# Feed-forward in front of an attention block: where eight 768 KB copies of constant rows are issued

## The chip, the cores and the metric

The kernel runs on one core of one Trainium2 chip. The metric is device time in microseconds (us), taken per execution. The time of before is the median of three runs. A profile comes from one further execution; its span leaves out a little of what the device time holds.

## What is computed

The input x is four sequences of 512 tokens of 128 numbers. The reference runs two layers of the form feed-forward, attention, feed-forward. The change lies in the first block of the first layer:

```
x = x + 0.5 * L0_ffn(layernorm(x))
x = x + L0_attn(layernorm(x))
...
```

`L0_ffn` sends each token to one of eight experts. The router takes a softmax over eight logits and the largest one wins. The chosen expert computes `gelu(t @ w1[e] + b1[e]) @ w2[e] + b2[e]`, which is multiplied by the winner's probability. `L0_attn` has 16 heads of 8 numbers with relative positions: besides q·k the scores get terms that depend on the distance of query and key in blocks of 64. The far part of these terms is put into the matmul: each head's q and k get 24 further rows. Some of them are the same for every input, zeros and ones that mark blocks of positions ("constant rows").

## The kernel before, in words

`network` (L2442) runs the phases in order. `constants_phase` starts the loads of x. `ffn_phase` (L306, its tiles are named l0f) is the first feed-forward. `relative_attend` (l0am) is the attention. Then come the second feed-forward, and the spline and causal phases of layer 1.

`ffn_phase` has two parts. In the first, the router: VectorE (DVE) normalises and ranks the 2048 tokens, and GpSimd (POOL) writes them sorted by expert to the DRAM tensor `sorted_tokens`, with 16 indirect DMAs (L499), then eight more that blank the rows past each expert's last token (L504). In the second part 23 slots of 128 tokens are worked through. For each slot s:

- SyncE (SP) reads the slot's row from SBUF (`packed_of`, L415), then copies the expert's w1 to `mine` (`load_mine`, L461, 256 KB) and loads the slot's tokens into `xs` (`load_tokens`, L471, 64.5 KB). For the first eight slots `load_tokens` waits for the slot's blanking DMA (`blanked[s]`).
- TensorE (PE) transposes the tokens (L872), does four "up" products (L882) and later four "down" products (L893). ScalarE (ACT) applies gelu (L593). DVE copies (L764) and adds the bias (L774), POOL writes the result to `token_results` (L509).

SP issues `mine` and `xs` four slots ahead (AHEAD = 4). The first four are outside the loop, the loop's body s issues those of slot s + 4.

While this phase runs, the attention's weights are prepared (`AttentionWeights`, the argument `aside`, tiles l0w). SP loads them behind the expert weights (`aside.load`, L953). PE, DVE and ACT form `wext` and `row_bias` between router and slots (`multiply`, L977: L981 to L1000). SP also stores the constant rows: `store_blocks` (L961) is one DMA from DRAM to DRAM of 16 heads x 24 rows x 512 numbers, 768 KB, for one sequence and side (q or k). There are eight, B = 4 sequences x 2 sides. The kernel before issues one at the end of the loop's bodies 0 to 7. `store_edges` (L969) follows behind the loop. The attention waits for all ten at L1237, behind its first row products.

The DMAs that SP issues share one queue (q1), on the same 16 DMA engines as POOL's indirect ones (q0). The order of the work is written out by hand: each engine runs its instructions in the order of the code and waits on semaphores.

Of the kernel before, what the change touches and what calls it, by code (L numbers as in the profile page):

```python
# [15 lines left out]
B, S, D = 4, 512, 128  # L16
# [289 lines left out]
def ffn_phase(nc, kept, name, x, arrivals, consts, w, scratch_dram, aside=None, late=None, closing=None):  # L306
# [4 lines left out]
    with ExitStack() as ctx:  # L311
        own_sems = []

        def sb(n, shape, dt=F32):
            return ctx.enter_context(nc.sbuf_tensor(f"{name}_{n}", shape, dt))
# [13 lines left out]
            return [sem(f"{n}{j}") for j in range(UNROLL)]  # L329

        SETS = TILES // 4
        experts = sb("experts", [P, EXPERTS, SLAB])
        mine = sb("mine", [P, UNROLL, FF])
        b1 = sb("b1", [EXPERTS * FC, P])
# [17 lines left out]
        onehot_b = sb("onehot_b", [P, TILES, EXPERTS], BF16)  # L352
        next_row = sb("next_row", [P, SETS, EXPERTS])
        place = sb("place", [P, TILES, EXPERTS])
# [58 lines left out]
        def packed_of(engine, s):  # L413

            return engine.value_load(packed_i[0:1, s:s + 1], min_val=0, max_val=EXPERTS * (XS_ROWS - P) + EXPERTS - 1)  # L415

        def row_of(packed):
            return (packed >> OWNER_BITS).with_bounds(max_val=XS_ROWS - P)

        def part_of(packed, at, n):  # L420
            expert = (packed & (EXPERTS - 1)).with_bounds(min_val=0, max_val=EXPERTS - 1)
            return experts[:, bass.ds(expert, 1), at:at + n].rearrange("p a k -> p (a k)")

        def load_results(queue, first, end):

            for j in range(UNROLL):
                queue.wait_ge(ys_out[j], 16 * len(range(j, SLOTS, UNROLL)))
            for b in range(first, end):
                queue.dma_start(yg[:, 4 * b:4 * b + 4, :], ys_dram[512 * b:512 * b + 512, :].rearrange("(t p) d -> p t d", p=P))\
                    .then_inc(gathered[b], 16)  # L430

        with nc.Block() as block:

            @block.sync
            def _(sp):
                sp.dma_start(switch_w[:, :], w["switch_w"]).then_inc(switch_in, 16)
                sp.dma_start(switch_b[:, :], w["switch_b"].unsqueeze(0).partition_broadcast(P)).then_inc(switch_in, 16)
                loads = [
                    (b1[:, :], w["b1"].rearrange("e (k p) -> (e k) p", p=P)),
                    (experts[:, :, SLAB_W1:SLAB_W2], w["w1"].rearrange("e d f -> d e f")),  # L440
                    (experts[:, :, SLAB_B2:SLAB_B1], w["b2"].unsqueeze(0).partition_broadcast(P)),
                ]
                for dst, src in loads:
                    sp.dma_start(dst, src).then_inc(weights_in, 16)
                for e in range(EXPERTS):
                    sp.dma_start(experts[:, e, SLAB_W2:SLAB_B2].rearrange("p (k d) -> p k d", k=FC),
                                 w["w2"][e].rearrange("(k p) d -> p k d", p=P)).then_inc(weights_in, 16)
                if aside:
                    aside.load(sp)
                if late:  # L450
                    late.load(sp)
                sp.wait_ge(weights_in, FFN_LOADS * 16)
                sp.wait_ge(b1_ready, 1)
                sp.wait_ge(rows_ready, 1)

                def load_mine(s, row):

                    j = s % UNROLL
                    if s >= UNROLL:
                        sp.wait_ge(up_ready, s - UNROLL + 1)  # L460
                    sp.dma_start(mine[:, j, :], part_of(row, SLAB_W1, FF)).then_inc(mine_in[j], 16)  # L461

                def load_tokens(s, row):

                    j = s % UNROLL
                    if s < EXPERTS:
                        sp.wait_ge(blanked[s], 16)
                    if s >= UNROLL:
                        sp.wait_ge(xsT_psum, s - UNROLL + 1)
                        sp.wait_ge(tokens_ready, s - UNROLL + 1)  # L470
                    sp.dma_start(xs[:, j, 0:XS_COLS], xs_dram[bass.ds(row_of(row), P), :]).then_inc(xs_in[j], 16)  # L471

                rows = [packed_of(sp, s) for s in range(AHEAD)]
                for s in range(AHEAD):
                    load_mine(s, rows[s])
                if arrivals:
                    sp.wait_ge(arrivals[1], 16)
                sp.wait_ge(scattered, 16 * TILES)
                for s in range(AHEAD):
                    load_tokens(s, rows[s])  # L480
                for s in range(SLOTS):
                    if s + AHEAD < SLOTS:
                        row = packed_of(sp, s + AHEAD)
                        load_mine(s + AHEAD, row)
                        load_tokens(s + AHEAD, row)
                    if aside and s < 2 * B:
                        aside.store_blocks(sp, s)
                if aside:
                    aside.store_edges(sp)
                load_results(sp, 0, B // 2)  # L490
# [110 lines left out]
            def _(dve):  # L601
# [126 lines left out]

                last_rows = next_row[:, SETS - 1, :]
                done(dve.tensor_scalar(blank_pos[:, :], last_rows, c["own_row"][:, 0:1], None, ALU.add))  # L730
# [1711 lines left out]
def network(nc, inputs, out, tables):  # L2442

    def weights(prefix, *more):
        names = {n[len(prefix):]: a for n, a in inputs.items() if n.startswith(prefix)}
        return {**names, **{n: tables[n] for n in more}}


    sorted_tokens = nc.dram_tensor("sorted_tokens", (XS_ROWS, XS_COLS), F32).ap()
    token_results = nc.dram_tensor("token_results", (YS_ROWS, D), F32).ap()  # L2450
    with ExitStack() as ctx:
        x = ctx.enter_context(nc.sbuf_tensor("x_tokens", [P, TILES, D], F32))
        c, x_in, empty_out = constants_phase(nc, ctx, x, inputs["L0_attn_hidden_states"], sorted_tokens)
        attention_w, dram = weights("L0_attn_", "own_head", "block_rows"), attention_dram(nc)
        closing = AttentionClosing(nc, ctx, "l0a", x, c, attention_w)
        with ExitStack() as attention_ctx:
            aside = AttentionWeights(nc, attention_ctx, "l0w", c, attention_w, dram)
            with aside.scratch():
                ffn_phase(nc, ctx, "l0f0", x, (x_in, empty_out), c, weights("L0_ffn_"), (sorted_tokens, token_results), aside)
            relative_attend(nc, ctx, "l0am", x, closing.xn, closing.heads, c, aside, closing.weights, dram)  # L2460
        layer1 = LayerOneWeights(nc, ctx, "l1w", c, weights("L1_ffn_"), weights("L1_attn_", "cos_rows", "sin_rows"))
        with layer1.scratch():
            ffn_phase(nc, ctx, "l0f1", x, None, c, weights("L0_ffn_"), (sorted_tokens, token_results), None, layer1, closing)
        spline_phase(nc, "l1f0", x, c, layer1)
        causal_phase(nc, "l1a", x, c, layer1)
        spline_phase(nc, "l1f1", x, c, layer1, out)
# [19 lines left out]
```

## Time and profile before

| what | us |
|---|---|
| median of 3 runs (788.44 to 790.29) | 788.75 |
| the profiled execution's own time | 788.52 |
| its span | 786.8 |
| PE busy over the span | 583.0 |
| DVE busy | 531.2 |
| ACT busy | 437.1 |
| POOL busy | 219.6 |

Times of an instruction or a stretch are us from the span's start. A row of the timeline gives start, duration, engine, line, operation, output and inputs, count, and in brackets the idle time before it with what ended it. SPq stands for the issuing of DMAs by SP: its duration is the issuing, not the transfer. In the rows of stretches a bracket (x4) counts instructions, PEclk is the granted TensorE clock as a share of 2.4 GHz, and the DMA share is the mean busy share of the core's 16 DMA engines (it can pass 1, as packets overlap).

### The profile page before, as it was taken

The numbers are of one execution on the slowest core, as the hardware profiler recorded it, in microseconds if no ns is written. First come the engines' busy times: TensorE is split into PE (matmuls) and PEld (weight loads), VectorE is DVE, ScalarE is ACT, GpSimd is POOL, SyncE is SP. The second block draws the span as 40 slices with busy tenths as digits, with TensorE's granted clock in tenths as the row PEclk, the third lists the DMA queues.
The fourth block names the chain that finished last, engine by engine and source line by source line (L and its number), as shares of the span: only waits on it lengthen the run. The fifth ranks groups of instructions, "written<-read, shape, count | busy, mean of one in ns | idle before, by whom it ended". The sixth has DMA issues, their size and how long they took to land. (4 is left out here: it accounts for less than half of the span.)

```text
span 786.8 us, 16609 instructions
## 1 busy us (share of the span) xinstructions
PE 583.0 (74%) x5220; PEld 417.2 (53%) x5220; DVE 531.2 (68%) x1878; ACT 437.1 (56%) x944; POOL 219.6 (28%) x274
## 2 busy tenths in 40 slices
PE   4499927727999999999999998343993661686660
PEld 3387923324666566667666666233982451364460
DVE  7612235815787678989999995771226888766887
ACT  2034524415888788888888884631551523464522
POOL 1743422000950391095040000056442100212000
PEclk9999977866999999999999998655997655799655
DMA  8669525989989899999954413725552000000001
GB/s 251 179 182 391 185 79 169 289 342 269 283 274 335 220 278 348 324 225 271 338 157 129 124 48 99 165 76 146 180 166 71 0 1 1 0 1 2 0 1 53
DMA packets 133602, 130.79 MB, mean 166 GB/s; under 512 B 29565, under 2 KB 109485, under 8 KB 131853
## 3 DMA queue, kind: packets, MB, share of 16 engines
q1 hardware_dynamic: 126668, 103.61, 46.3%
q0 software_dynamic: 4736, 25.07, 8.7%
q10 hardware_dynamic: 2112, 1.05, 0.5%
q8 instruction: 44, 0.72, 0.4%
q14 instruction: 42, 0.34, 0.1%
HBM read 73.43 MB, written 52.92 MB: 161 GB/s over the span
## 5 line engine op out<-in xcount | busy, mean ns | idle before, releaser
L1442 DVE CUSTOM_DVE_ANT_0 l0am_prob<-l0am_ps_s,l0am_bias 128x512 f32<-128x512 f32 x256 | 161.6, 687 | 56.1 <-PE l0am_ps_s L1519 34.9
L1361 ACT ACTIVATE l0am_prob<-l0am_prob,l0am_neg_top 128x512 f32<-128x512 f32 x256 | 172.1, 730 | 19.1 <-DVE l0am_neg_top L1442 19.0
L1531 PE MATMUL l0am_ps_t<-c_ident,l0am_prob 128*128 128x128 f32 x1024 | 138.2, 279 | 0.0
L1531 PEld LDWEIGHTS l0am_ps_t<-c_ident,l0am_prob 128*128 128x128 f32 x1024 | 113.8, 142 | 16.7 <-issue 16.6
L1355 ACT COPY l0am_probT<-l0am_ps_t 128x512 f32<-128x512 f32 x128 | 69.0, 590 | 45.6 <-PE l0am_ps_t L1531 45.6
L1519 PE MATMUL l0am_ps_s<-l0am_ks,l0am_qs 32*128 32x512 f32 x512 | 74.0, 647 | 21.7 <-DVE l0am_neg_top L1442 19.5
L1429 DVE COPY l0am_probT<-l0am_ps_t 128x512 f32<-128x512 f32 x128 | 82.2, 683 | 2.5 <-PE l0am_ps_t L1531 2.4
L764 DVE COPY l0f_xsT<-l0f_psT 128x128 f32<-128x128 f32 x46 | 13.4, 292 | 97.5 <-PE l0f_psT L872 97.5
L593 ACT ACTIVATE l0f_h<-l0f_psU,l0f_experts 128x128 f32<-128x128 f32 x184 | 52.6, 368 | 47.2 <-PE l0f_psU L882 47.2
L1544 PE MATMUL l0am_ps_c<-l0am_probT,l0am_v 128*9 128x128 f32 x2048 | 67.9, 273 | 0.9 <-issue 0.9
L509 POOL DMA_INDIRECT token_results<-l0f_ys,l0f_token_i x46 | 44.3, 962 | 62.5 <-DVE l0f_ys L774 61.9
L882 PE MATMUL l0f_psU<-l0f_xsT,l0f_mine 128*128 128x128 f32 x368 | 55.3, 297 | 4.2 <-issue 1.8
L1142 POOL TENSOR_TENSOR l0am_near<-l0am_rows_q,l0am_rows_k 128x352 f32<-128x352 f32 (+7 forms) x24 | 31.3, 1336 | 96.2 <-DMA l0am_rows_k<-position_k 86.8
L1544 PEld LDWEIGHTS l0am_ps_c<-l0am_probT,l0am_v 128*9 128x9 f32 x2048 | 49.5, 90 | 11.7 <-issue 11.6
L1151 POOL TENSOR_TENSOR l0am_near<-l0am_rows_q,l0am_rows_k 128x192 f32<-128x192 f32 (+6 forms) x96 | 54.0, 608 | 0.2
L882 PEld LDWEIGHTS l0f_psU<-l0f_xsT,l0f_mine 128*128 128x128 f32 x368 | 48.6, 206 | 8.3 <-issue 4.9
L499 POOL DMA_INDIRECT sorted_tokens<-l0f_xn,l0f_pos_i x32 | 31.4, 980 | 56.7 <-DVE l0f_pos_i L665 47.9
L1519 PEld LDWEIGHTS l0am_ps_s<-l0am_ks,l0am_qs 32*128 32x128 f32 x512 | 20.2, 184 | 47.8 <-issue 25.4
L1552 PEld LDWEIGHTS l0am_ps_g<-c_ident,l0am_headT 128*128 128x128 f32 x64 | 9.0, 140 | 48.2 <-issue 28.8
L1481 PE MATMUL l0am_ps_s<-l0am_xnT,l0w_wext 128*112 128x512 f32 (+1 forms) x48 | 27.2, 726 | 4.5 <-ACT l0am_rows L1337 3.8
L893 PE MATMUL l0f_psR<-l0f_experts,l0f_h 128*128 x192 | 27.1, 286 | 1.7 <-ACT l0f_h L593 1.7
L1337 ACT ACTIVATE l0am_rows<-l0am_ps_s,l0w_row_bias 112x512 f32<-112x512 f32 (+1 forms) x24 | 16.1, 687 | 20.6 <-PE l0am_ps_s L1481 7.2
(312 smaller groups left out, 976.6 us busy)
## 6 DMA issues: line engine op xcount, KB each, us to landing
l0am_bias<-near_terms SPq DMA_DIRECT2D x128, 192.0 KB, 4.8
near_terms<-l0am_near POOLq DMA_DIRECT2D x12, 1536.0 KB, 8.3
l0f_mine<-l0f_experts SPq DMA_DIRECT2D x46, 256.0 KB, 2.8
l0am_rows_k<-position_k SPq DMA_DIRECT2D x16, 448.0 KB, 6.9
near_terms<-l0am_near SPq DMA_DIRECT2D x1, 6144.0 KB, 19.8
position_q<-l0am_rows SPq DMA_DIRECT2D x20, 224.0 KB, 4.8
position_k<-l0am_rows SPq DMA_DIRECT2D x20, 224.0 KB, 4.9
l0am_rows_q<-position_q SPq DMA_DIRECT2D x20, 224.0 KB, 6.0
```

Of the source, the lines that this page charges most:

```text
L499: pool.indirect_dma_start(xs_dram[:, :], bass.IndirectOffsetOnAxis(ap=pos_i[:, t:t + 1], axis=0), xn[:, t, 0:XS_COLS], None).then_inc(scat ...
L509: pool.indirect_dma_start(ys_dram[:, :], bass.IndirectOffsetOnAxis(ap=token_i[:, s:s + 1], axis=0), ys[:, s % UNROLL, :], None).then_inc(y ...
L593: last = nc.scalar.activation(h[:, j, k, :], psU[:, s % 2, k, :], ACT.Gelu_apprx_tanh, bias=part_of(row, SLAB_B1 + k, 1))
L882: last = pe.matmul(psU[:, s % 2, k, :], mine[:, j, k * P:(k + 1) * P], xsT[:, j, :], start=True, stop=True)
L1151: last = engine.tensor_tensor(view(near, at, (WIN + 1, 64), (1, width)), view(rows_q, ROW_OF[pq] * 64, (1, 64), (0, width)), view(rows_k, ...
L1355: nc.scalar.copy(probT[:, u // GROUP % 2, u % GROUP, :, :], ps_t[:, u % 2, :, :]).then_inc(copied_act, 1)
L1361: nc.scalar.activation(prob[:, k, :], prob[:, k, :], ACT.Exp, bias=neg_top[:, k:k + 1], scale=-1.0)\
L1429: dve.tensor_copy(probT[:, u // GROUP % 2, u % GROUP, :, :], ps_t[:, u % 2, :, :]).then_inc(copied_dve, 1)
L1442: dve.tensor_tensor_reduce(out=prob[:, k, :], in0=ps_s[:, j, :], in1=bias[:, j, at:at + S], scale=-1.0, scalar=HUGE, op0=ALU.add, op1=ALU.min,
L1519: pe.matmul(ps_s[:, j, :], qs[r, n % 2, t * P:t * P + P], ks[r, n % 2, :], start=True, stop=True, tile_position=(32 * j, 0)).then_inc(scor ...
L1531: last = pe.transpose(ps_t[:, u % 2, i, :], prob[:, u % SLOTS_, i * P:(i + 1) * P], ident[:, :])
L1544: last = pe.matmul(ps_c[32 * j:32 * j + DH + 1, 0:P], v[:, T4 * b + i, GROUP * g + j, :], probT[:, q % 2, j, i, :], start=(i == 0), stop=( ...
```

## The change

Six of the eight copies are issued right behind the loads of the weights, before SP waits for anything. The other two stand at the end of the loop's bodies 10 and 14.

```diff
@@ -329,6 +329,7 @@
         SETS = TILES // 4
+        EARLY_BLOCKS, LATE_BLOCKS = 2 * B - 2, (10, 14)
         experts = sb("experts", [P, EXPERTS, SLAB])
@@ -447,6 +448,8 @@
                 if aside:
                     aside.load(sp)
+                    for n in range(EARLY_BLOCKS):
+                        aside.store_blocks(sp, n)
                 if late:
                     late.load(sp)
                 sp.wait_ge(weights_in, FFN_LOADS * 16)
@@ -483,8 +486,8 @@
                         load_mine(s + AHEAD, row)
                         load_tokens(s + AHEAD, row)
-                    if aside and s < 2 * B:
-                        aside.store_blocks(sp, s)
+                    if aside and s in LATE_BLOCKS:
+                        aside.store_blocks(sp, EARLY_BLOCKS + LATE_BLOCKS.index(s))
                 if aside:
                     aside.store_edges(sp)
```

Only SP's order changes. Behind the loads of the attention's weights stood, before, the reads of the first slots' rows (`l0w_` are the attention's weights, `stacked_` the tensors that take the constant rows):

```order
L959 DMA l0w_wv<-in_L_attn_Wv 128x128
L959 DMA l0w_bv<-in_L_attn_bv 128x128
L415 TENSOR_LOAD l0f_packed_i
L415 ISA x2
L415 TENSOR_LOAD l0f_packed_i
```

In the changed kernel the same place reads:

```order
L962 DMA l0w_wv<-in_L_attn_Wv 128x128
L962 DMA l0w_bv<-in_L_attn_bv 128x128
L970 DMA stacked_q<-in_block_rows 16x24x512
L970 DMA stacked_k<-in_block_rows 16x24x512
L970 DMA stacked_q<-in_block_rows 16x24x512
L970 DMA stacked_k<-in_block_rows 16x24x512
L970 DMA stacked_q<-in_block_rows 16x24x512
L970 DMA stacked_k<-in_block_rows 16x24x512
L416 TENSOR_LOAD l0f_packed_i
```

Six DMAs of 768 KB now go ahead of the `mine` and `xs` loads of all slots in SP's queue. In the loop, the bodies 0 and 1 on SP read before:

```order
L461 DMA l0f_mine<-l0f_experts 128x512
L471 ISA
L471 DMA l0f_xs<-sorted_tokens 128x129
L967 DMA stacked_q<-in_block_rows 16x24x512
L415 TENSOR_LOAD l0f_packed_i
L415 ISA x2
L461 REGISTER_ALU
L461 ISA
L461 DMA l0f_mine<-l0f_experts 128x512
L471 ISA
L471 DMA l0f_xs<-sorted_tokens 128x129
L967 DMA stacked_k<-in_block_rows 16x24x512
```

and now:

```order
L464 DMA l0f_mine<-l0f_experts 128x512
L474 ISA
L474 DMA l0f_xs<-sorted_tokens 128x129
L416 TENSOR_LOAD l0f_packed_i
L416 ISA x2
L464 REGISTER_ALU
L464 ISA
L464 DMA l0f_mine<-l0f_experts 128x512
L474 ISA
L474 DMA l0f_xs<-sorted_tokens 128x129
```

The store between two bodies is gone in bodies 0 to 7. Bodies 10 and 14 get one each.

## Rows read from the trace of the kernel before

**Rows 1.** Busy time by stretch: us, engines, granted clock, DMA share, GB/s
```profile
27.00:40.00 13.00, 6.08 (x12) 2.98 (x13) 7.08 (x32) 0.89 (x2) 9.89 (x11) 1.00 0.41 138
40.00:46.00 6.00, 5.91 (x26) 5.20 (x24) 0.00 (x0) 0.89 (x2) 4.54 (x5) 1.00 0.30 71
...
55.70:81.80 26.10, 23.57 (x173) 20.30 (x172) 5.63 (x30) 11.43 (x40) 9.58 (x10) 1.00 1.01 366
...
81.80:99.80 18.00, 17.82 (x156) 17.40 (x155) 5.21 (x27) 10.29 (x36) 8.43 (x9) 1.00 0.49 167
```
**Rows 2.** Timeline of PE: transposes of slots 0, 4, 13 and 22
```profile
46.28 0.45 PE L872 MATMUL l0f_psT<-c_ident,l0f_xs 128*128 128x128 f32 x1
...
57.67 0.27 PE L872 MATMUL l0f_psT<-c_ident,l0f_xs 128*128 128x128 f32 x1
...
81.79 0.27 PE L872 MATMUL l0f_psT<-c_ident,l0f_xs 128*128 128x128 f32 x1
...
99.77 0.27 PE L872 MATMUL l0f_psT<-c_ident,l0f_xs 128*128 128x128 f32 x1
```
**Rows 3.** DMA issues between 55 and 81 us: count, size, median us to landing
```profile
l0f_mine<-l0f_experts SPq DMA_DIRECT2D x11, 256.0 KB, 7.0
stacked_q<-in_block_rows SPq DMA_DIRECT2D x3, 768.0 KB
...
l0f_xs<-sorted_tokens SPq DMA_DIRECT2D x10, 64.5 KB, 6.6
token_results<-l0f_ys,l0f_token_i POOLq DMA_INDIRECT x10, 5.4
```
**Rows 4.** DMA issues between 81 and 106 us
```profile
l0f_mine<-l0f_experts SPq DMA_DIRECT2D x7, 256.0 KB, 2.4
l0f_xs<-sorted_tokens SPq DMA_DIRECT2D x7, 64.5 KB, 1.9
token_results<-l0f_ys,l0f_token_i POOLq DMA_INDIRECT x14, 2.2
```
**Rows 5.** Timeline of SP's issuing, first feed-forward
```profile
8.41 12.88 SPq L446 DMA_DIRECT2D l0f_experts<-in_L_ffn_w  x8
...
25.30 0.43 SPq L959 DMA_DIRECT2D l0w_bv<-in_L_attn_bv  x1
35.26 2.60 SPq L461 DMA_DIRECT2D l0f_mine<-l0f_experts  x4
42.78 4.56 SPq L471 DMA_DIRECT2D l0f_xs<-sorted_tokens  x4
...
48.87 0.40 SPq L471 DMA_DIRECT2D l0f_xs<-sorted_tokens  x1
...
70.22 0.62 SPq L967 DMA_DIRECT2D stacked_k<-in_block_rows  x1
...
72.67 0.35 SPq L471 DMA_DIRECT2D l0f_xs<-sorted_tokens  x1
...
95.40 0.36 SPq L471 DMA_DIRECT2D l0f_xs<-sorted_tokens  x1
```
**Rows 6.** Waits of SP between 25 and 75 us: total, times, longest
```profile
SPq L454 <- DVE l0f_experts L755: 6.8, 1, 6.8
```
**Rows 7.** Timeline of POOL: last scatter, first blanking
```profile
38.98 0.96 POOL L499 DMA_INDIRECT sorted_tokens<-l0f_xn,l0f_pos_i  x1 [0.31 <-issue]
40.24 0.96 POOL L504 DMA_INDIRECT sorted_tokens<-c_blank,l0f_blank_i  x1 [0.30 <-issue]
```
**Rows 8.** Timeline of PE and DVE: the attention's weights, ahead of the slots
```profile
29.13 0.48 PE L981 MATMUL l0w_ps<-c_ident,l0w_wq 128*128 128x128 f32 x1 [1.99 <-DMA l0w_bv<-in_L_attn_bv]
...
32.44 0.48 DVE L1010 COPY l0w_turned_w<-l0w_ps 128x320 f32<-128x320 f32 x1
...
43.72 2.70 PE L1000 MATMUL l0w_ps<-l0w_bk,l0w_pext 128*128 128x1 f32 x12
```
**Rows 9.** Timeline of PE: an "up" group of slot 0 and of slot 3
```profile
47.12 2.08 PE L882 MATMUL l0f_psU<-l0f_xsT,l0f_mine 128*128 128x128 f32 x8 [0.39 <-DVE l0f_xsT L764]
...
56.78 1.06 PE L882 MATMUL l0f_psU<-l0f_xsT,l0f_mine 128*128 128x128 f32 x8
```
**Rows 10.** Timeline of PE, second feed-forward: transposes of slots 0, 3 and 22
```profile
542.31 0.47 PE L872 MATMUL l0f_psT<-c_ident,l0f_xs 128*128 128x128 f32 x1 [13.93 <-DMA l0f_xs<-sorted_tokens]
...
550.59 0.27 PE L872 MATMUL l0f_psT<-c_ident,l0f_xs 128*128 128x128 f32 x1
...
590.63 0.27 PE L872 MATMUL l0f_psT<-c_ident,l0f_xs 128*128 128x128 f32 x1
```

## The prediction

> **What bounds the kernel now.** I read the busy time by stretch first, to find where the eight stores run. Between 55.7 and 81.8 us the DMA engines' share is 1.01 at 366 GB/s; after the last store has drained it is 0.49 at 167 GB/s; and ahead of the slots, from 27 to 46 us, it is 0.41 and then 0.30 [rows 1]. So the stores run while the DMA engines have nothing to spare, and a stretch in which they are more than half idle lies right before. PE's timeline says what that costs: from slot 4 to slot 13 nine slots take 81.79 - 57.67 = 24.12 us, 2.68 each; from slot 13 to slot 22 nine take 99.77 - 81.79 = 17.98 us, 2.00 each [rows 2]. The DMA issues give the reason: a slot's w1 copy lands 7.0 us after its issue instead of 2.4, its tokens 6.6 instead of 1.9 [rows 3, 4], and SP issues them only four slots ahead. Nothing else changes between the two stretches; PE is the bound in the second. The slots are on the path of the whole kernel: the attention needs every token's result, and no later phase starts before.
>
> SP is close to a bound too. Without stores it needs (95.40 - 72.67) / 10 = 2.27 us a slot from one tokens' load to the next [rows 5], more than PE's 2.00. A store adds 0.62 us of issuing, so with stores SP needs 2.9, the same as one slot's 1.1 MB at full DMA rate. Both bounds go when the stores go.
>
> **The change part by part.**
>
> *Taken out of bodies 0 to 7.* The slots 4 to 13 go at 2.00 us instead of 2.68: 24.12 - 17.98 = 6.1 us gained. The second feed-forward, the same code with no stores, goes from slot 3 to slot 22 in 40.04 us, 2.11 a slot [rows 10]; by that rate the nine slots would gain 5.1. I take 6.1 and keep 5.1 as the other end. Slots 0 to 4 gain nothing: two of their slots run with PE groups twice as long (2.08 us against 1.06 [rows 9]), and no store is ahead of their loads.
>
> *Six stores at 25.7 us.* SP issues them between 25.73 and about 29.7 us (6 x 0.66, from 0.62 and the gap). Before, SP waited there 6.8 us, until 32.5 [rows 6], so up to 2.8 us more of issuing cost SP nothing. The transfers are 6 x 0.786 = 4.7 MB. The DMA work already in 27 to 40 us takes a share of 0.41, so 0.6 of the engines is free there, and 0.7 from 40 to 46. At 366 GB/s for a share of 1.01 the stores alone need 13 us of full share; 13 x 0.6 = 7.8 are served by 40 us, the other 5 take until 47. At a somewhat better rate for 2 KB rows it would be 44. The queue is thus full until **about 45 us**, with the four w1 copies of 35.26 us behind the stores in it.
>
> What is late then? The preparation of the attention's weights is not: their last load is ahead of the stores, PE takes it at 29.13, and its three transposes are waited for by a copy that DVE starts only at 32.44, busy until then [rows 8]. Some 2.3 us of lateness are covered; beyond that each us would count. The w1 copies are wanted at 47.12 [rows 9] and land about 45. The tokens are not covered: slot 0's load waits for the first blanking, issued by POOL at 40.24 [rows 7], and SP went on at 42.78 [rows 5], 2.5 us later. POOL's indirect DMAs landed in 2.2 us with the engines half idle and in 5.4 with them full [rows 3, 4]. So the blanking lands at 40.24 + 5.4 = 45.6, the tokens' load is issued there and lands into a queue that has just emptied: 3.0 us, between 1.9 and 6.6. PE transposes slot 0 at about 48.8 instead of 46.28, where it came right behind the last bias products, which end at 46.4 [rows 8]. There was no slack. **Loss: 2.5 us**; the ends are 0 (the queue empties before 41 us) and 40.24 + 5.4 + 6.6 - 46.28 = 6.0.
>
> The page "DMA: Bandwidth & Descriptors" of the Trainium skill, section "Latency and other measured facts", gives HBM access as 0.2 us on average and 2 us at high load. By it the blanking and the tokens would be late by some 1.8 us each way at the worst; an estimate from that page is a start 1.8 to 3.6 us late, and the sum would be a gain of 2.5 to 4.3.
>
> *Two stores in bodies 10 and 14.* Tokens of slot 14 go out at 50.2 + 10 x 2.27 = 73 us (50.2 is worked out below), those of slot 18 at 83, and a store behind each. The free share beside the slots is 0.5 [rows 1], so the 2.1 us of a store are absorbed in two slots, and the loads run four slots ahead. I take nothing. The other end is the price of a store now, 6.1 / 8 = 0.8 us each, 1.5 together. SP's side: tokens of slot 4 went out at 48.87, now at about 50.2, since slots 1 to 3 catch up with POOL's beat of 1.26 us. Eighteen slots at 2.27 and two stores at 0.66 bring slot 22 to 92.4, and 1.9 to landing gives 94.3. PE's own side is 57.67 + 2.5 + 18 x 2.00 = 96.2. PE bounds, by 1.9 us.
>
> *Behind the slots* nothing moves: the attention's wait for the ten stores comes behind its first row products, long after the last store, which now goes out at 83 instead of 70.22 [rows 5].
>
> **The sum.** 6.1 - 2.5 - 0 = 3.6 us: slot 22 at 96.2 instead of 99.77. Against the profiled execution's 788.52 this is **784.9 us**. The median of the runs is 788.75, 0.2 above it. What a measurement tells from no change is 0.3%, 2.4 us: faster means below 786.4, slower above 791.1.
>
> **The rivals.**
>
> *The start is not late.* If the stores go faster than I reckon, or POOL's DMAs hardly suffer, slot 0 still starts at 46.3 and all 6.1 us stay: 782.4. For it: POOL's DMAs have a queue of their own, and four fifths of the stores may be through when the blanking comes. Against it: the 5.4 us of the loop, where they had the same queue [rows 3]. Chance 0.25.
>
> *The start eats the gain.* Blanking and tokens both land as slowly as in the loop, and the start is 6.0 us late: 788.4. A start 3.7 us late is enough to fall inside the 2.4 us. For it: the w1 copies stand behind the stores and ahead of the tokens. Against it: in the loop the tokens are behind a store and a copy each time, here the queue has emptied. Chance 0.12.
>
> *The low clock lasts longer.* PE would now stand idle for 2.4 us between bias products and slot 0. Its groups are at the low level (1.2 GHz by their 2.08 us, though the granted clock's column shows 1.00) in the first slots and at 2.4 GHz by slot 3 [rows 9]. If the rise comes a slot later for the idle time, two groups cost 2.0 us more: 786.9. Against it: the second feed-forward starts out of 13.9 us of idle, and its slot 3, 8.3 us after the start, is transposed in 0.27 us, fast; here slot 4 is the first of the rows that is, 11.4 us after the start [rows 2, 10]. The page "TensorE: Matmul & The Clock Gate" of the Trainium skill, part 1, says that the low clock is the default and sustained activity releases it, which puts the gap on the side of this cost. Chance 0.05.
>
> *SP is held by its own stores: slower.* The eight w2 loads took SP 12.88 us to issue, 1.6 each: a full queue holds the issuer [rows 5]. If the stores hold SP until the queue is empty, at 45 us, its wait ends there instead of at 32.5. From there to the first tokens' load it needs at least 37.86 - 32.5 = 5.4 us, four rows read and four w1 copies issued [rows 5, 6]. The tokens go out at 50.4, slot 0 starts at 53.7, 7.4 us late. With 1.5 us for the two late stores: 788.5 + 7.4 + 1.5 - 6.1 = 791.3. The point from which it is slower than before is SP held beyond 42 us. Against it: a store in the loop was issued in 0.62 us with the engines full [rows 5]. Chance 0.06.
>
> That the change does not do what it says is excluded by the order of SP's instructions; nothing else moved.
>
> **How the numbers follow.** My case, a start 1.2 to 3.7 us late and 783.6 to 786.1, has 0.52; no late start 0.25; an eaten gain 0.12; the longer low clock 0.05; slower 0.06. The first two give faster: 0.77. The next two give no change: 0.17. Range: from 782.0, the full 6.1 us and 0.4 for the clock or the median's 0.2, to 787.3, a start 4.9 us late, which takes in the longer low clock and half of the eaten gain. About 0.12 lies above it, little below.
>
> **What would show it.** In the new profile: the share between 30 and 44 us near 1, and about 0.5 to 0.6 from 50 to 72; SP's wait at its first wait shorter by 4 us, its six stores issued by 30 to 31; the tokens of slot 0 issued at 45 to 46; PE's first transpose at 48 to 49.5; slots 4 to 13 in 18 to 19 us; slot 22 at 95 to 97. A first transpose at 46.3 means the first rival; at 51 or later, the second or third, told apart by whether SP's issuing rows of the stores are long. I am wrong about the cause if the slots keep 2.7 us without the stores.

## The result, and the profile after

| | us |
|---|---|
| before, median of 5 runs | 788.75 (787.26 to 790.29) |
| after, median of 5 runs | 792.68 (791.77 to 792.99) |
| after, the profiled execution and its span | 792.71 and 791.0 |

The ratio is 1.0069 (95% interval 1.0037 to 1.0101): the change makes the kernel **slower**, by some 4 us. The prediction was 784.9 us (782.0 to 787.3), with a chance of 0.06 for slower.

PE's timeline of the changed kernel, with the last bias products and the transposes of slots 0, 4, 13 and 22, is the counterpart of [rows 2, 8]:

```profile
44.47 1.48 PE L1003 MATMUL l0w_ps<-l0w_bk,l0w_pext 128*128 128x1 f32 x12
56.84 0.48 PE L875 MATMUL l0f_psT<-c_ident,l0f_xs 128*128 128x128 f32 x1 [10.89 <-DMA l0f_xs<-sorted_tokens]
...
68.34 0.27 PE L875 MATMUL l0f_psT<-c_ident,l0f_xs 128*128 128x128 f32 x1
...
86.66 0.27 PE L875 MATMUL l0f_psT<-c_ident,l0f_xs 128*128 128x128 f32 x1
...
104.61 0.27 PE L875 MATMUL l0f_psT<-c_ident,l0f_xs 128*128 128x128 f32 x1
```

Slot 0 starts at 56.84 instead of 46.28: 10.6 us late, where I had 2.5. PE waits 10.89 us for the tokens. Slots 4 to 13 take 86.66 - 68.34 = 18.32 us instead of 24.12, which is the expected gain (5.8 of 6.1), and slots 13 to 22 take 17.95, as before. One late store falls into each of the two stretches (issued at 79.29 and 89.42). Slot 22 is at 104.61, 4.8 us later than before, and the second feed-forward's slot 0 is transposed at 546.40, 4.1 later than before [rows 10].

About 2 us of the 10.6 lie ahead of the change's place. POOL issues its first scatter at 21.53 us, before at 19.57. That is five us ahead of the first store, so the stores are not its cause. From there POOL keeps its beat of 1.26 us:

```profile
21.53 1.18 POOL L502 DMA_INDIRECT sorted_tokens<-l0f_xn,l0f_pos_i  x1 [16.67 <-DVE l0f_pos_i L668]
...
40.95 0.96 POOL L502 DMA_INDIRECT sorted_tokens<-l0f_xn,l0f_pos_i  x1 [0.30 <-issue]
42.22 0.96 POOL L507 DMA_INDIRECT sorted_tokens<-c_blank,l0f_blank_i  x1 [0.30 <-issue]
```

The profiles of the experiments have the first scatter anywhere from 19.3 to 21.1, whatever the kernel. So from here on I count slot 0 from the first scatter: 46.28 - 19.57 = 26.7 us before, 56.84 - 21.53 = 35.3 after. The change's own lateness is **8.6 us**, and slot 22, counted in the same way, is 2.9 us late. The medians differ by 3.9.

SP's issuing, the counterpart of [rows 5], shows where the tokens stood:

```profile
30.73 2.69 SPq L970 DMA_DIRECT2D stacked_k<-in_block_rows  x1
37.29 5.19 SPq L464 DMA_DIRECT2D l0f_mine<-l0f_experts  x4
50.33 3.52 SPq L474 DMA_DIRECT2D l0f_xs<-sorted_tokens  x4
```

and its waits between 24 and 62 us [rows 6]:

```profile
SPq L470 <- DMA sorted_tokens<-c_blank,l0f_blank_i: 7.6, 1, 7.6
SPq L474 <- DMA sorted_tokens<-c_blank,l0f_blank_i: 1.2, 2, 0.8
SPq L457 <- DVE l0f_experts L758: 1.1, 1, 1.1
```

SP issued the sixth store by 33.4 us (four of the six took 0.62 to 0.87, the last 2.69). It was held a little, but went on before the blanking was even issued; its long wait is the one for the blanking, 7.6 us. The blanking went out at 42.22 and SP's load of the tokens at 50.33: 8.1 us later, where it was 40.24 to 42.78, 2.5 us, before [rows 5, 7]. The tokens then took from 50.33 to 56.84. The DMA issues of 36 to 44 us:

```profile
l0f_mine<-l0f_experts SPq DMA_DIRECT2D x4, 256.0 KB, 16.9
...
sorted_tokens<-c_blank,l0f_blank_i POOLq DMA_INDIRECT x2, 7.7
```

and of 50 to 54 us:

```profile
l0f_xs<-sorted_tokens SPq DMA_DIRECT2D x4, 64.5 KB, 6.2
```

One reason stands in the stretches of the changed kernel, four us each:

```profile
26.00:30.00 4.00, 0.90 (x13) 0.66 (x12) 3.25 (x20) 0.23 (x1) 3.09 (x4) 1.00 0.57 98
30.00:34.00 4.00, 0.98 (x3) 0.47 (x3) 3.54 (x17) 0.00 (x0) 3.09 (x4) 1.00 1.00 333
34.00:38.00 4.00, 1.08 (x3) 0.89 (x4) 2.67 (x10) 0.00 (x0) 3.09 (x4) 1.00 1.06 247
38.00:42.00 4.00, 3.91 (x6) 1.62 (x6) 0.00 (x0) 0.89 (x2) 3.00 (x4) 1.00 1.06 250
42.00:46.00 4.00, 3.80 (x27) 3.09 (x25) 0.00 (x0) 0.84 (x3) 2.88 (x3) 1.00 1.12 246
46.00:50.00 4.00, 0.00 (x0) 0.00 (x0) 0.00 (x0) 0.16 (x1) 3.07 (x4) 0.52 0.96 296
50.00:54.00 4.00, 0.00 (x0) 0.00 (x0) 0.00 (x0) 0.00 (x0) 1.73 (x2) 0.50 1.04 332
54.00:58.00 4.00, 0.78 (x2) 0.48 (x3) 0.35 (x2) 0.00 (x0) 0.00 (x0) 0.50 0.74 206
```

From 34 to 46 us a full share carries only 246 to 250 GB/s, where I had reckoned with 366 [rows 1], and the engines stay full until about 55 us instead of 45. Blanking and tokens both go out inside that stretch. The w1 copies suffer too: they land 16.9 us after their issue, the first at about 54 us, not much ahead of the tokens.

The other reason lies in POOL's own queue, q0. The blanking stands there behind the 16 scatters, of 32 packets each. From 28 to 32 us, as the stores begin, that queue moves next to nothing. Its rows (packets, MB, share of the engines) of these four us, before and after:

```profile
q0 software_dynamic: 129, 0.26, 19.3%
q0 software_dynamic: 18, 0.04, 2.6%
```

and from the first scatter to the issue of the first blanking, 19.5 to 40.2 us before and 21.5 to 42.2 after:

```profile
q0 software_dynamic: 475, 0.99, 14.4%
q0 software_dynamic: 373, 0.79, 13.9%
```

When the blanking goes out, POOL's queue is 102 packets, some three scatters, further behind than before. From 36 to 44 us it moves 0.39 MB, no more than POOL adds in that time (66 KB every 1.26 us), so it does not catch up while the engines are full.

PE is idle for 10.9 us and its granted clock falls to 0.50, the lower of its two levels (1.2 GHz). Slots 0 to 4 take 68.34 - 56.84 = 11.5 us, 11.4 before [rows 2], so the longer idle time added nothing to them. The start before was no warm one, though: its last bias products took 2.70 us [rows 8], against 1.48 now, so by this time PE was at the low level already there (though the granted clock's column shows 1.00), and slot 0 waited for them until 46.28, some 1.5 us after its tokens had landed (a load of 2.0 us from 42.78).

In us: 5.6 for the blanking (8.1 - 2.5) and 3.0 for the tokens (6.5 from SP's issue to the transpose instead of 3.5) make 8.6 of lateness, less 5.8 in the slots and with the 2.0 ahead of it: slot 22 is 4.8 later.

### The profile page after: what moved, and what is told of

Same layout as the page of the kernel before. It is cut to its first block and busy times, and to the rows that moved or that the text cites. A ratio compares the mean times of both kernels' runs of the same rounds, so it can differ in the third digit from the quotient of the medians.

```text
span 791.0 us, 16609 instructions
## 1 busy us (share of the span) xinstructions
PE 582.0 (74%) x5220; PEld 417.3 (53%) x5220; DVE 531.8 (67%) x1878; ACT 436.6 (55%) x944; POOL 220.0 (28%) x274
## 3 DMA queue, kind: packets, MB, share of 16 engines
q10 hardware_dynamic: 2112, 1.05, 0.5%
## 5 line engine op out<-in xcount | busy, mean ns | idle before, releaser
L1534 PEld LDWEIGHTS l0am_ps_t<-c_ident,l0am_prob 128*128 128x128 f32 x1024 | 114.3, 143 | 16.7 <-issue 15.8
L1555 PEld LDWEIGHTS l0am_ps_g<-c_ident,l0am_headT 128*128 128x128 f32 x64 | 9.0, 141 | 49.1 <-issue 29.6
L875 PE MATMUL l0f_psT<-c_ident,l0f_xs 128*128 128x128 f32 x46 | 13.7, 297 | 25.0 <-DMA l0f_xs<-sorted_tokens 24.8
L1484 PE MATMUL l0am_ps_s<-l0am_xnT,l0w_wext 128*112 128x512 f32 (+1 forms) x48 | 29.1, 774 | 3.7 <-ACT l0am_rows L1340 3.0
```

What stands on the lines that cost most here:

```text
L1534: last = pe.transpose(ps_t[:, u % 2, i, :], prob[:, u % SLOTS_, i * P:(i + 1) * P], ident[:, :])
```

## The experiments

**Theory A**: the six stores keep the DMA engines full until about 55 us, the blanking and the tokens land late through it, and the start's lateness grows with the number of early stores. **Rivals**: SP itself is held by its stores; the order in SP's own queue (w1 copies behind stores) is what delays. The length of the low clock is dealt with above.

All kernels are given as changes to the changed kernel. The five groups fall under two conditions of the chip. In two (before at 788.81 and 789.17 us) it was as in the profiles above. In the other three (before at 809.13, 810.88 and 808.65) every kernel took some 20 us more: between about 28 and 55 us PE, ACT and SP stood still for some 11 us before slot 0, which I call held signals. I tell the undisturbed groups first, since only they show the start. The kernel before has one profile, of the undisturbed kind.

### How many stores are early

Eight early; and two early, three directly behind the loads of the last slot, three behind the loads of the results:

```diff
-        EARLY_BLOCKS, LATE_BLOCKS = 2 * B - 2, (10, 14)
+        EARLY_BLOCKS, LATE_BLOCKS = 8, ()
```

> All eight stores early. Theory A (each early store keeps the queue full about 2.4 us longer, and the tokens of slot 0 land only when it is empty): on a chip with no held signals (kernel before near 789 us) slot 0 starts 4 to 5 us later than in the changed kernel, at 60 to 62 us, and the time is 1.008 to 1.014 of before. On a chip like the two of the first eight runs (kernel before near 810 us, where SP issues its first w1 copy only at 52 to 55 us) the queue is full until 55 us instead of 50, and slot 0 starts 0 to 3 us later than the change's 59. Rival E (SP, held by its own stores, is what is late, and not the transfers): SP's first w1 copy goes out later by the issuing of the two stores, 3 us or more.

```diff
-        EARLY_BLOCKS, LATE_BLOCKS = 2 * B - 2, (10, 14)
+        EARLY_BLOCKS, LATE_BLOCKS = 2, ()
...
+                    for n in range(2, 5):
+                        aside.store_blocks(sp, n)
                 if aside:
                     aside.store_edges(sp)
                 load_results(sp, 0, B // 2)
+                if aside:
+                    for n in range(5, 2 * B):
+                        aside.store_blocks(sp, n)
```

> Two early, three behind the last slot's token load, three behind the loads of the results, a second time. Theory A: the engines' share is back at 0.5 or below by 38 us, slot 0 waits for nothing that the stores move, and the time is below before's: 0.990 to 0.995 on a chip near 789 us, 0.993 to 0.999 on one near 810 us, where it was 0.996.

Measured in one group, before at 788.81: eight early 794.58 us, ratio 1.0092 (1.0060 to 1.0123); two early 781.12 us, **0.9904 (0.9873 to 0.9934)**, faster than both kernels. PE's slot 0 with eight early:

```profile
61.14 0.48 PE L875 MATMUL l0f_psT<-c_ident,l0f_xs 128*128 128x128 f32 x1 [17.39 <-DMA l0f_xs<-sorted_tokens]
```

Its stretches, full until 62 us:

```profile
42.00:46.00 4.00, 1.74 (x16) 1.66 (x15) 0.00 (x0) 0.17 (x1) 3.08 (x4) 0.79 1.01 222
46.00:50.00 4.00, 0.00 (x0) 0.00 (x0) 0.00 (x0) 0.00 (x0) 2.87 (x4) 0.50 1.07 265
...
58.00:62.00 4.00, 0.48 (x2) 0.19 (x2) 0.35 (x2) 0.00 (x0) 0.00 (x0) 0.50 1.06 356
```

And SP, which is now held by its stores:

```profile
31.51 3.35 SPq L970 DMA_DIRECT2D stacked_q<-in_block_rows  x1
34.90 3.85 SPq L970 DMA_DIRECT2D stacked_k<-in_block_rows  x1
41.74 5.62 SPq L464 DMA_DIRECT2D l0f_mine<-l0f_experts  x4
49.12 4.24 SPq L474 DMA_DIRECT2D l0f_xs<-sorted_tokens  x4
```

Counted from the first scatter the w1 copies go out at 22.4 us instead of 15.8, but the tokens at 29.8 instead of 28.8: what shrinks is the wait for the blanking, to 1.5 us. SP still ends by waiting for the blanking, which lands in 8.9 us, and the tokens then take 12 us. So SP's being held is not what delays the tokens. With two early the stretches are:

```profile
30.00:34.00 4.00, 1.13 (x4) 0.61 (x4) 3.43 (x15) 0.00 (x0) 3.09 (x4) 1.00 0.99 383
34.00:38.00 4.00, 2.03 (x4) 1.20 (x5) 1.81 (x6) 0.00 (x0) 3.08 (x4) 1.00 0.54 189
...
42.00:46.00 4.00, 3.07 (x25) 2.94 (x25) 0.00 (x0) 0.35 (x2) 2.94 (x4) 0.87 0.26 70
```

The stores are through by 36 us, at 383 GB/s; the engines are three quarters idle when the blanking goes out, and POOL's queue has caught up (475 packets from the first scatter to the blanking's issue, as before). The blankings land in 2.9 us and the tokens in 2.2, both as before. Slot 0 is at 45.77, and slot 22, with the slots free of stores, at 94.49 instead of 99.77.

### Queue, source and number, in one group

The changed kernel once more, and three variants, before at 789.17. The changed kernel:

> The changed kernel, once more in search of an execution without held signals (kernel before near 789 us). Theory A there: slot 0 at 54 to 57 us, time 1.003 to 1.010 of before. With held signals: slot 0 at 59 to 60, time 0.997 to 1.001.

792.69 us, 1.0046 (1.0012 to 1.0080): the slower result again. Slot 0 waits 11.43 us for the tokens; the rate in a full share is 226 to 251 GB/s from 34 to 46 us.

Four early, four behind the loads of the results:

```diff
-        EARLY_BLOCKS, LATE_BLOCKS = 2 * B - 2, (10, 14)
+        EARLY_BLOCKS, LATE_BLOCKS = 4, ()
...
+                if aside:
+                    for n in range(4, 2 * B):
+                        aside.store_blocks(sp, n)
```

> Four early, four behind the results. Without held signals, theory A: the stores are through at 42 us and the w1 copies behind them at 44; the blanking lands 4 to 6 us after its issue, slot 0 starts at 48 to 51 us, between the 45.8 of two early stores and the change's, and the time is 0.992 to 0.998 of before. With held signals: 0.993.

786.07 us, 0.9954 (0.9921 to 0.9988). Between two and six, as theory A has it: full until 46 us, SP goes on 6.1 us after the blanking's issue (41.79 to 47.88). POOL's queue is as far behind at that issue as in the changed kernel (384 packets), but the stores are nearly through, and from 44 to 48 us it moves 0.37 MB and catches up. Its stretches and slot 0:

```profile
42.00:46.00 4.00, 3.45 (x24) 3.36 (x24) 0.00 (x0) 0.47 (x3) 3.09 (x4) 0.77 1.04 371
46.00:50.00 4.00, 0.00 (x0) 0.00 (x0) 0.00 (x0) 0.00 (x0) 3.08 (x4) 0.50 0.60 145
```

```profile
50.76 0.48 PE L878 MATMUL l0f_psT<-c_ident,l0f_xs 128*128 128x128 f32 x1 [5.17 <-DMA l0f_xs<-sorted_tokens]
```

The six early stores issued by ScalarE, into its own queue, behind its work for the router:

```diff
-                    for n in range(EARLY_BLOCKS):
-                        aside.store_blocks(sp, n)
...
                 if aside:
+                    for n in range(EARLY_BLOCKS):
+                        aside.store_blocks(act, n)
                     aside.copy(act)
```

> The six early stores in ScalarE's queue. Without held signals, theory F (order in one queue): w1 copies land in 3 to 6 us instead of 17, tokens in 3 to 4 instead of 6, slot 0 at 51 to 53 us. Theory G (full engines): slot 0 within 1 us of the change's. With held signals nothing can be told, as the queue is empty before SP's first copy.

789.40 us, 1.0002 (0.9972 to 1.0031). SP is no longer held by stores (its w1 copies are issued at 35.69 in 2.58 us, as before [rows 5]) and no store is ahead of them in its queue. Yet the start is as late. SP's wait, the queues from 36 to 44 us, and slot 0:

```profile
SPq L468 <- DMA sorted_tokens<-c_blank,l0f_blank_i: 10.4, 1, 10.4
```

```profile
q10 hardware_dynamic: 745, 1.46, 68.3%
q0 software_dynamic: 218, 0.45, 21.3%
q1 hardware_dynamic: 199, 0.38, 15.3%
...
sorted_tokens<-l0f_xn,l0f_pos_i POOLq DMA_INDIRECT x4, 7.5
sorted_tokens<-c_blank,l0f_blank_i POOLq DMA_INDIRECT x3, 8.1
```

```profile
56.15 0.47 PE L875 MATMUL l0f_psT<-c_ident,l0f_xs 128*128 128x128 f32 x1 [11.68 <-DMA l0f_xs<-sorted_tokens]
```

The blanking lands in 8.1 us though no store is in its queue, and SP's four w1 copies (1.05 MB), alone in q1, have moved 0.38 MB by 44 us. So the order in SP's queue is not what delays; the 16 engines, which all the queues share, are full. The order in POOL's own queue does count: the last four scatters, in front of the blanking, need 7.5 us themselves, and by the blanking's issue the queue had moved 382 packets, about as in the changed kernel.

The six early stores read from the blank tile in SBUF, three rows of each store by one partition, and the other two stand behind the loads of the results. This kernel's constant rows so have other values, in all its runs:

```diff
+        if n < 6:
+            dst = bass.AP(self.dram["stack"][side].tensor, MARGIN + (b * HEADS * 32 + 8) * FAR_PITCH,
+                          [(32 * FAR_PITCH, HEADS), (3 * FAR_PITCH, 8), (FAR_PITCH, 3), (1, S)])
+            src = self.blank[:, :, :].rearrange("p a c -> p (a c)")[:, 0:3 * S].rearrange("p (r s) -> p r s", r=3)
```

> Six early stores from SBUF, two behind the results (constant rows get other values). Theory D, now with a measured rate of 320 GB/s against 250: without held signals slot 0 starts at 50 to 53 us, 3 to 5 us ahead of the change. With held signals as last time: 0.992 of before.

787.23 us, 0.9975 (0.9942 to 1.0008), a clear miss for the start: slot 0 comes at 54.41, where 50 to 53 was expected. The rate did rise, to 300 to 331 GB/s from 34 to 46 us:

```profile
34.00:38.00 4.00, 2.03 (x4) 1.09 (x5) 1.81 (x6) 0.00 (x0) 3.09 (x4) 1.00 1.02 331
38.00:42.00 4.00, 3.53 (x12) 1.78 (x10) 0.00 (x0) 1.69 (x4) 3.07 (x4) 1.00 1.02 311
42.00:46.00 4.00, 2.81 (x21) 2.73 (x20) 0.00 (x0) 0.17 (x1) 2.88 (x3) 0.70 0.98 300
```

but the tokens go out no earlier. SP's stores take 2.0 us each to issue from the third on, and the w1 copies come at 42.86 instead of 36.30 and hold it until 48.79:

```profile
33.45 1.98 SPq L979 DMA_DIRECT2D stacked_k<-c_blank  x1
42.86 5.93 SPq L464 DMA_DIRECT2D l0f_mine<-l0f_experts  x4
49.49 3.75 SPq L474 DMA_DIRECT2D l0f_xs<-sorted_tokens  x4
```

Its wait behind that is still one for the blanking:

```profile
SPq L470 <- DMA sorted_tokens<-c_blank,l0f_blank_i: 0.4, 1, 0.4
```

SP is held, as the prediction's fourth rival has it, but the blanking comes even later: issued at 41.02, it lands in 8.2 us, at 49.2. POOL's queue was as far behind here as in the changed kernel (368 packets by the blanking's issue), and a rate of 300 GB/s and more did not let it catch up. What the faster source gave is the tokens' time, 4.9 us from issue to transpose instead of 6.35 and 6.5. What it would give with SP not held the kernel doesn't tell.

The undisturbed kernels together. "Start" is slot 0's transpose less the first scatter, "end" is slot 22's less the first scatter, the last two columns are against before (of the profiles, and of the medians of the same group):

| early stores | start | end | end against before | median against before |
|---|---|---|---|---|
| none (before) | 26.7 | 80.2 | | |
| 2 | 25.3 | 74.1 | -6.1 | -7.7 |
| 4 | 29.6 | 76.4 | -3.8 | -3.1 |
| 6, from SBUF | 34.1 | 81.3 | +1.1 | -1.9 |
| 6 (the change) | 35.3 | 83.1 | +2.9 | +3.9 |
| 6 (again) | 35.9 | 82.7 | +2.5 | +3.5 |
| 6, ScalarE's queue | 36.2 | 82.9 | +2.7 | +0.2 |
| 8 | 41.8 | 87.4 | +7.2 | +5.8 |

The first two stores cost the start nothing, the third and fourth 4.3 us together, the fifth and sixth 6, the seventh and eighth 6. At 3 us a store (0.79 MB at 250 GB/s) each pair should cost 6, and it does once the engines are still full when the blanking goes out. Each row is one profile, and the start before carries some 1.5 us of waiting for its slow bias products, which would explain the 1.4 that two early stores seem to gain.

Two medians, of ScalarE's queue and of SBUF, lie 2.5 and 3 us below what the profiles' slots give; that is open. The intervals of the ratios are about 2.5 us to either side, and what follows slot 22 took 686.4 us in one profile of the changed kernel and 689.2 in the other, so differences of this size are not told from noise.

### The groups with held signals

In these the start says nothing of the stores. This is the timeline of PE with all eight stores behind the loads of the results, where no store runs before 113 us and the DMA share is 0.18 from 28 to 40 us:

```profile
42.77 2.07 PE L999 MATMUL l0w_ps<-l0w_pext,l0w_turned_w 128*128 128x512 f32 x2 [6.13 <-remote]
...
57.75 0.45 PE L878 MATMUL l0f_psT<-c_ident,l0f_xs 128*128 128x128 f32 x1
```

First group, before at 809.13. All eight behind (the edit as with four early, with 0), two early with six behind, four early, and six from SBUF:

> All eight stores are issued behind the loads of the first feed-forward's results, none ahead of or among the slots. Theory A (the early stores keep the DMA queue full until 55 us, and the blanking and the tokens of slot 0 land late because of it): slot 0 is transposed 3 us or less behind the end of the last bias products (it was 10.9 us behind them in the changed kernel), slots 4 to 22 go at 2.0 us each, and slot 22 is at 94 to 96 us against 104.6 in the change and 99.8 before. The eight stores need some 17 us of the queue from 103 us on; the attention's first row stores come at about 118 and may wait 0 to 3 us. Time 782 to 786. Theory B (the late start has nothing to do with the stores: other traffic or a different draw of the run): slot 0 stays at 56 us, time 787 or more.

> Two stores early, six behind the loads of the results. Theory A: two stores take 2 x 0.786 MB at the 285 GB/s measured beside POOL's scatters, 5.5 us, so the queue is empty before 38 us, the blanking lands 2.5 us after its issue as before, and slot 0 starts where the bias products end, at 46 to 48.5 us. Time as with all behind, 782 to 786. Theory C (DRAM to DRAM copies hurt POOL's scatters whatever their number, since a scatter that is held up once holds all behind it): slot 0 starts 2 us or more late, at 50 us or later, and the time is 2 us or more above that with all behind.

> Four stores early, four behind the loads of the results. Theory A: the queue is full until about 55 - 2 x 2.5 = 50 us less what is saved as the scatters are undisturbed earlier, so about 47 us; the blanking lands 3 to 5 us after its issue and slot 0 starts at 49 to 52 us, about half of the ten us that six stores cost. Time 784 to 788. If the delay jumps only with the fifth store (SP held, which began with the fourth store's issue of 0.87 us), slot 0 starts at 46 to 48 us, as with two.

> Six stores early as in the change, two behind the loads of the results; the six read 1536 numbers per partition of a constant tile in SBUF instead of DRAM, to the same addresses with the same row length of 2 KB. The constant rows get other values in this kernel; no work is left out. Theory D (what makes the stores slow beside the scatters, 285 GB/s instead of 366, is that they read and write DRAM at once): they move at 350 GB/s or more, the queue is empty at about 46 us, and slot 0 starts at 48 to 51 us. Theory A in its plain form (the bytes and packets in the queue count, wherever they come from): the queue is full until about 53 to 55 us and slot 0 starts at 54 to 57.

811.07 us, 1.0014 (0.9983 to 1.0045), slot 0 at 57.75; 806.81, 0.9974 (0.9946 to 1.0003), 58.12; 806.01, 0.9961 (0.9930 to 0.9992), 60.31; and one run at 806.82, 59.84. With all stores behind, slot 22 is at 103.81 but nothing is won: from 117 to 130 us the DMA share is 1.02 at 346 GB/s, where the attention's first copies want the engines. So the stores seem not to be free behind the slots either; no profile of before with held signals is there to say how much they cost. The kernel with the split issue puts three of them beside the last slots instead.

Second group, before at 810.88: the changed kernel, all behind, two early split as above, SBUF.

> The changed kernel itself, beside the next ones on one chip. On the chip of the first four runs PE and ACT were held for some 11 us by late signals between 30 and 52 us (kernel before 809 us instead of 789), so that slot 0 began at 57 to 60 us in all four, whatever the stores. Theory A: where those signals are not late, slot 0 is at 54 to 57 us and waits for its tokens' DMA; the time is 1.003 to 1.010 of before. Where they are late again, the change's late tokens are hidden behind them and the gain in the slots shows: 0.990 to 0.998 of before.

> All eight stores behind the loads of the results. Theory A: slot 0 starts where the bias products end (at 46 to 48.5 us if no signal is late), slot 22 at 94 to 96, and the DMA work of the attention's start takes back 0 to 5 us, as the near terms' store and loads and the eight stores share 110 to 180 us, where the engines' share rose from 0.75 to 0.92 in the first run of this kernel. Time 0.992 to 1.000 of before. Theory B (the late start is not the stores' doing): slot 0 at 55 us or later without any late signal.

> Two stores early, three directly behind the last slot's token load, three behind the loads of the results. If theory A holds, the two early ones are through by 38 us and cost nothing, the three behind the loop run from 92 to 100 us beside the last slots, whose loads are ahead of them, and the last three are through at about 114 us, before the attention's row stores. It should be the fastest of all: 0.990 to 0.994 of before without late signals. If two early stores do cost (theory C), slot 0 begins 2 us or more after the bias products.

> Six stores early that read a constant tile in SBUF instead of DRAM, two behind the results; the constant rows get other values. Theory D (DRAM to DRAM is what makes them slow beside the scatters): the engines move 350 GB/s or more while they run, the queue is empty by 46 us and slot 0 starts 5 us or more earlier than in the changed kernel. Theory A in its plain form: slot 0 within 2 us of the changed kernel's. On the first chip the stores' rate can be compared alone: the stretch of full share was 25 us long in the changed kernel.

810.42 us, 0.9994 (0.9969 to 1.0020); 812.79, 1.0021 (0.9993 to 1.0049); 806.83, 0.9962 (0.9929 to 0.9994); 809.30, 0.9988 (0.9957 to 1.0020). Slot 0 at 58.91, 58.61, 61.07 and 61.57.

Third group, before at 808.65: the changed kernel, SBUF, ScalarE's queue, four early.

> The changed kernel once more, for slot 0's start without a held signal. Theory A: slot 0 at 54 to 57 us (one profile had 56.8, with everything from 12 us on 2 us late by a later load of the router's bias; without that, 55), tokens' loads issued at 47 to 50 and landing 6 us later. With eight stores early it was 61.1, with two 45.8. Time 1.003 to 1.010 of before. If the signals are held (before near 810 us): slot 0 at 58 to 59 as in both kinds of kernel.

> Six stores early that read SBUF, two behind the results (constant rows get other values). In the two runs with held signals these stores moved at 290 to 320 GB/s beside the scatters and the queue was empty at 46 us; the change's moved at 250 GB/s and it was empty at 50. So for theory D (DRAM to DRAM beside the scatters sets the rate): slot 0 starts 3 to 5 us earlier than in the changed kernel, at 50 to 53 us, and the time is 0.993 to 1.000 of before. For the plain count of bytes: the same start as the change within 1 us.

> The change, but the six early stores are issued by ScalarE behind its last exponentials, into its own queue instead of SP's; the two late ones stay on SP. Theory F (the tokens and w1 copies are late because they stand behind the stores in one queue): the w1 copies land in 3 to 6 us instead of 17, the tokens in 3 to 4 instead of 6, slot 0 starts 2 to 4 us earlier than in the change, the blanking still lands 7 us after its issue. Theory G (the engines are full, and whoever uses them is late): the tokens take 6 us and slot 0 starts within 1 us of the change's.

> Four early, four behind the results. Theory A: from two early stores (slot 0 at 45.8) to eight (61.1), each store beyond what 27 to 40 us can take costs 2.5 to 3 us; the change's six give 54 to 57, so four give 48 to 51 us. The queue is empty at 43 us (in the run with held signals its share fell to 0.3 there). Time 0.992 to 0.999 of before.

807.05 us, 0.9977 (0.9941 to 1.0013); 802.74, 0.9918 (0.9883 to 0.9954); 804.56, 0.9940 (0.9913 to 0.9967); 805.07, 0.9933 (0.9903 to 0.9963). Slot 0 at 59.75, 57.60, 63.81 and 59.93.

All the expectations on the start that were made for an undisturbed chip missed here: slot 0 is at 57 to 64 us in every kernel, in no order of early stores. What reads through is the time at which the engines come free, with the w1 copies not yet issued: about 36 us with two early, 42 to 43 with four, 49 with six, 46 with six from SBUF. That supports theory A's first half. Where the start is late anyway, the change loses nothing and four early, or two and a split, still win 3 to 4 us, and six from SBUF 6 in one of three groups.

## Why the prediction was wrong

- *The bound of before, and the gain in the slots*: right. 5.8 us against 6.1, both by PE's transposes; the low rate of the slots was the stores'.
- *Two late stores for nothing*: right within 0.4 us. The second falls into slots 13 to 22, which take 17.95 us against 17.98, though w1 copies land in 3.6 us there instead of 2.4 [rows 4]; the first falls into slots 4 to 13, which take 18.32.
- *The preparation of the attention's weights is covered*: right. Its last products end at 45.95 us in the new profile, and nothing waits for them.
- *The low clock does not last longer*: right, 11.5 us for slots 0 to 4 against 11.4, after 10.9 us of idle where I had 2.4. In the repeat of the changed kernel they took 9.9. The start before was at the low level too, so this compares two cold starts.
- *SP held by its own stores*: the last store took 2.69 us to issue, so the mechanism is there, but its long wait is the one for the blanking. With eight stores it was held 3.85 us by the last and still ended by waiting for the blanking.
- **"At 366 GB/s for a share of 1.01 the stores alone need 13 us of full share ... The queue is thus full until about 45 us"**: this is the step that failed. The engines carried 246 to 250 GB/s at a full share for 12 us. With 333 before and 296 behind it they came free at about 55 us. From 30 to 54 us they moved 6.8 MB, which at 366 GB/s would have been through at 49 us, so some 6 of the ten us are the rate. The rest was in my own terms: the plain sum gave 47, I took 45 for a better rate that no row showed, and the first store went out at 26.68 instead of 25.73. The 366 were measured where a store came every 2.9 us among copies of w1, which then landed in 7.0 us [rows 3]; behind six stores issued in one go they took 16.9. The alternative I named was a *better* rate for 2 KB rows; a worse one was not in the bounds. Why the rate is lower stays open.
- *The blanking lands in 5.4 us, the tokens in 3.0*: wrong, in part a consequence. I took the loop's value for the blanking and an emptied queue for the tokens. The engines were full for both, and the blanking took 7.8 us, the tokens 6.2. The loop's value also left out that the blanking stands behind POOL's scatters, which the stores had already set back by some three. I had held "the start eats the gain" at 6.0 us as the outer end; it was 8.6. The w1 copies, which I had landing at about 45 us, landed at about 54.
- *Two slips that changed little*: 45.6 + 3.0 is 48.6 and not 48.8; and "there was no slack" was a misreading, as slot 0 waited some 1.5 us for the bias products and not for its tokens.
- *The case "slower"* was given SP's issuing as its mechanism. What came true was another priced rival, the start that eats the gain, pushed past its bound: the bounds came from the loop, where the backlog was smaller.

The page "DMA: Bandwidth & Descriptors" of the Trainium skill, section "Latency and other measured facts", gives HBM access as 2 us at high load, and the estimate from it was a start at most 3.6 us late. The trace doesn't bear the estimate out: behind the backlog the blanking alone was 5.6 us later than before.

## What to carry to other kernels

A stretch where the DMA engines are idle is worth only what drains before the first short transfer on the path: work out when the backlog is gone with a rate of that kind of transfer in a row, not of a mixed stretch, and compare that time with the issue of the transfer that others wait for. Here two copies of 768 KB fit and each further one delayed the start by up to 3 us, more than the 0.7 us that it cost in the loop. A queue of its own did not protect a short transfer here, since the queues share the engines. And look at what stands in front of the short transfer in its own queue: the blanking was late also because the scatters ahead of it were.

## What the runs showed of the hardware that I had not expected

- **The engines carry less when copies from DRAM to DRAM pile up beside POOL's scatters.** With two early stores the engines carried 383 GB/s from 30 to 34 us; with six they reach about 400 for some 2 us and then carry 226 to 251 while the scatters run. With eight in a row behind the slots, where no scatter runs, they carried 346 GB/s (117 to 130 us, other copies among them). From SBUF the six went at 300 to 331 beside the scatters. Why is open.
- **A short DMA waits behind a backlog in any queue.** The blanking (about 64 KB) landed in 2.9 us with the engines mostly idle, 7.7 behind six stores, 8.9 behind eight, and 8.1 with the stores in a third queue; a 64.5 KB load of tokens in 2.2, 6.2 and up to 12.
- **POOL's queue nearly stops as a burst of stores begins.** From 28 to 32 us it moved 0.04 MB instead of 0.26, and with only two early stores 0.07. With two it made this up by 41 us (0.40 MB from 32 to 36 us); with six it did not before the blanking. Why is open.
- **Held signals.** On two chips (one of which gave undisturbed runs at another time) PE, ACT and SP stood still for some 11 us in all before slot 0, in waits that the trace ends by "remote" or "issue", while POOL issued its indirect DMAs. One wait of PE was 6.13 us, and the kernel before took 809 us instead of 789. It happened with the engines almost idle (share 0.18), so the early stores are not its cause. The cause is open.
